# The second half of a two-layer vision tower: another layout of attention, work moved from VectorE to ScalarE, gelu over pairs of banks

## What is computed

```python
# layer 1, after the first layer's attention and mixture of experts
h = h + attn(layernorm(h))       # 16 heads of 16, causal, no softmax:
    att = where(causal, q @ k.T / sqrt(16), -inf)
    att = (where(att > 0, att**2 + 1, 0) + where(-100 <= att <= 0, 1 - att/100, 0)) / 1000
    y = (att @ v) @ W_proj
h = h + ffn(layernorm(h))        # ternary weights w_up (1024x256), w_down (256x1024)
    up = gelu(rms_norm(x) @ ternary(w_up).T)
    out = rms_norm(up) @ ternary(w_down).T
```

## Time and profile before

| | us |
|---|---|
| median of 3 runs | 829.77 (825.41 to 830.24) |
| the profiled execution | 828.23 |
| its span, first to last instruction | 826.2 |
| busy: TensorE | 713.3 (86%) |
| busy: VectorE | 645.6 (78%) |
| busy: ScalarE | 406.4 (49%) |
| busy: GpSimd | 86.4 (10%) |

### The profile page before, as it was taken

The page is one execution under the profiler, slowest core; times in us unless marked ns, Lnnn a source line. Parts: engine busy times, 40 slices in busy tenths (PEclk is TensorE's granted clock), DMA queues, the critical chain, the costliest instruction groups (busy, mean ns, idle before and its releaser), DMA issues.

```text
span 826.2 us, 25282 instructions
## 1 busy us (share of the span) xinstructions
PE 713.3 (86%) x10749; PEld 508.4 (62%) x10749; DVE 645.6 (78%) x1444; ACT 406.4 (49%) x609; POOL 86.4 (10%) x76
## 2 busy tenths in 40 slices
PE   4878999999999999858776889999999988988756
PEld 3565767666666767545574566666666756655634
DVE  6677979797978788786596589888888998686753
ACT  4536464545555554543213573828456481745413
POOL 1100212121212120100000000010101010010000
PEclk9889999999999999957855999999999999999969
DMA  8033202020202002000000000000000000000000
GB/s 306 35 138 118 77 0 76 0 76 0 76 0 76 0 0 103 3 1 1 2 0 2 2 2 27 2 28 2 25 0 0 25 2 26 2 28 2 28 0 27
DMA packets 7532, 27.24 MB, mean 33 GB/s; under 512 B 2480, under 2 KB 3376, under 8 KB 5936
## 3 DMA queue, kind: packets, MB, share of 16 engines
q1 hardware_dynamic: 7472, 26.35, 8.7%
HBM read 22.16 MB, written 4.19 MB: 32 GB/s over the span
## 4 chain that ended last, share of the span: by engine, by line
PE 51%; DVE 24%; issue 10%; ACT 9%; SPq 2%; DMA 2%; POOL 1%; DVEq 0%; POOLq 0%; ACTq 0%
PE PS L374 8%; PE PS L753 6%; PE PS L323 5%; PE PS L385 5%; PE PS L718 4%; PE PS L484 4%; PE PS L364 4%; PE PS L473 3%; DVE mx L1308 3%; DVE Pm L1314 3%; PE PS L428 2%; ACT w_s L1029 2%; PE PS L695 2%; PE PS L709 2%; DVE work L1700 2%
## 5 line engine op out<-in xcount | busy, mean ns | idle before, releaser
L904 ACT ACTIVATE PT<-PS 128x512 f32<-128x512 f32 x64 | 36.8, 596 | 71.5 <-PE PS L473 71.5
L364 PE MATMUL PS<-ident_s,xn 128*128 128x128 f32 x256 | 48.1, 305 | 25.9 <-DVE xn L1229 22.7
L731 PE MATMUL PS<-xT,wqkv_h 128*128 128x512 f16 x256 | 63.8, 394 | 6.0 <-ACT w_s L1029 4.5
L323 PE MATMUL PS<-tokW_h,w_s 128*128 128x256 f16 x504 | 58.5, 273 | 0.0
L897 ACT ACTIVATE Pm<-Pm 128x1024 f32<-128x1024 f32 x32 | 33.1, 1054 | 46.5 <-DVE Pm L1314 46.5
L364 PEld LDWEIGHTS PS<-ident_s,xn 128*128 128x128 f32 x256 | 31.1, 149 | 38.4 <-DVE xn L1229 20.7
L323 PEld LDWEIGHTS PS<-tokW_h,w_s 128*128 128x128 f16 x504 | 48.7, 98 | 5.8
L753 PE MATMUL PS<-tokW_h,work 128*128 128x256 f16 x448 | 51.4, 273 | 0.3 <-issue 0.3
L374 PE MATMUL PS<-xT,wat_h 128*128 128x512 f16 x192 | 46.2, 400 | 4.5 <-DVE xT L1618 4.5
L731 PEld LDWEIGHTS PS<-xT,wqkv_h 128*128 128x128 f16 x256 | 22.7, 100 | 44.1 <-ACT w_s L1029 18.0
L473 PE MATMUL PS<-ident_s,Pm 128*128 128x128 f32 x256 | 42.5, 305 | 6.7 <-DVE Pm L1314 6.4
(11 more groups left out here) (248 smaller groups left out, 1605.7 us busy)
## 6 DMA issues: line engine op xcount, KB each, us to landing
work<-in_x SPq DMA_DIRECT2D x7, 1536.0 KB, 6.5
out<-H SPq DMA_DIRECT2D x8, 512.0 KB, 2.6
w_s<-in_w SPq DMA_DIRECT2D x3, 1024.0 KB, 7.0
work<-in_x SPq DMA_DIRECT2D x3, 512.0 KB, 6.1
wup_s<-in_wup SPq DMA_DIRECT2D x1, 1024.0 KB, 5.8
wdn_s<-in_wdn SPq DMA_DIRECT2D x1, 1024.0 KB, 7.9
w_s<-in_tokW SPq DMA_DIRECT2D x3, 256.0 KB, 4.5
wup_s<-in_wqkv SPq DMA_DIRECT2D x1, 768.0 KB, 7.5
```

The source lines that it names most:

```text
L323: m = pe.matmul(dst, halves_[xi][:, k, rows], w[:, wi, k, cols], start=(n == 0), stop=(n == 3 * chunks - 1))
L364: m = pe.transpose(PS[:, bank, t * P:(t + 1) * P], xn[:, t, c * P:(c + 1) * P], ident_s[:, :])
L731: m = pe.matmul(PS[:, UP_BANKS[f % 3], :], wup_h[:, c, f * P:(f + 1) * P], part[:, c, :], start=(k == 0), stop=(k == 2 * C - 1))
```

## The change

- Attention: keys are stored once (kT), the queries twice with zeros (qM), in the buffers exchanged. Scores are 32 rows by 64 columns (image_scores, as in the first half), with 128 moving columns; partitions are (image of the tile, key). The mask is 16 small matmuls a tile with the same tiles (keyb, cmaskb). Value products have depth 64, 64 for each pair of tiles in place of 32, into banks 4 and 5 by image. The value projection is one product of 128x256 a tile and pass.
- VectorE pieces on ScalarE: norm3 for slots 1 to 7 becomes a_norm3 (Identity with bias -mean*rstd and scale rstd; VectorE makes the bias, minus_mean3), turned becomes a_turned, the keys of v_B1 go to a_B1_k. ScalarE has them behind lins(g, 3), and the second a_turned behind the queries.
- silus(g) moves to slot g+1, behind minus_mean3.
- TensorE's down products of tiles 0 and 1 run their high halves ahead of the grams, their low halves behind them, all four tile halves in bank 7 (down_part).
- Gelu, copy and low half go over two banks at a time (1024 elements) for blocks 0 to 5, and singly for 6 and 7; four up banks in place of three.
- Setup: cmask comes in eight small loads at the end of loads_B in place of one at its head; setup_B makes keyb by a memset and two reductions in place of one copy.

```diff
-        UP_BANKS = (4, 7, 5)
+        UP_BANKS = (6, 7, 4, 5)
...
-        loads_B = [(cmask_s, cmask), (eb_s, eb), (rev8_s, rev8), (ridx_s, ridx), (iota_s, iota64),
+        loads_B = [(eb_s, eb), (rev8_s, rev8), (ridx_s, ridx), (iota_s, iota64),
...
+        loads_B += [(cmask_s[32 * i:32 * i + 32, :, 0:L], cmask[32:64, :, :]) for i in range(4)]
+        loads_B += [(cmask_s[32 * i:32 * i + 32, :, L:96], cmask[0:32, :, 0:32]) for i in range(4)]
...
             def turn2(g, last):
                 if last:
-                    pe.wait_ge(Bq_out, 2)
+                    pe.wait_ge(Bq_out, 4)
...
             def B2_scores(g, t):
-                for i in range(4):
-                    pe.matmul(PS[:, i, hb:hb + 256], identb[:, :], cmaskb[:, :, :], start=True, stop=False,
-                              skip_group_check=True)
-                for b in range(2):
...
-                            m = pe.matmul(PS[:, i, hb + c * P + b * L:hb + c * P + (b + 1) * L],
-                                          kB[r, c, 2 * t + b, :, :], qT[r, c, at:at + L],
-                                          start=False, stop=True, tile_position=(32 * i, 0), skip_group_check=True)
-                m.then_inc(Bs_mm, 1)
+                for upper in (True, False):
+                    qs = slice(0, L) if upper else slice(0, 32)
+                    at = slice(0, L) if upper else slice(L, 96)
+                    for b in range(2):
+                        for i in range(4):
+                            r = slice(32 * i, 32 * i + 32)
+                            masked = PS[b * L:(b + 1) * L, i, hb:hb + 256].rearrange("p (h q) -> p h q", q=L)
+                            pe.matmul(masked[:, :, qs], keyb[r, int(upper), :], cmaskb[r, :, at], start=upper,
+                                      stop=False, tile_position=(32 * i, b * L), skip_group_check=True)
+                image_scores(t, kT, qM, hb).then_inc(Bs_mm, 1)
...
             def B2_values(g, pair):
+                    for c in range(C):
+                        for e in range(2):
+                            for b in range(2):
+                                for i in range(4):
...
+                                    m = pe.matmul(PS[32 * i:32 * i + 32, 4 + b, to:to + L],
+                                                  V2[rows, t, 4 * i + 2 * c + e, :], F[rows, t % 2, at:at + L],
+                                                  start=(e == 0), stop=(e == 1), tile_position=(b * L, 32 * i),
+                                                  skip_group_check=True)
...
             def B3_up(g, nxt):
-                    if f >= 3:
-                        pe.wait_ge(g_ok, NF * g + f - 2)
+                    if f == 4:
+                        pe.wait_ge(g_ok, 5 * g + 1)
+                    elif f == 6:
+                        pe.wait_ge(g_ok, 5 * g + 2)
...
             def slot_B(g, prev, nxt, routed=None):
                 if prev:
-                    pe.wait_ge(g_ok, NF * g)
+                    pe.wait_ge(g_ok, 5 * g)
+                    for t in (0, 1):
+                        down_part(g - 1, t, G_hi, True)
                     for f in range(NF):
                         gram(g - 1, f)
-                    B3_down(g - 1, (0, 1))
+                    for t in (0, 1):
+                        down_part(g - 1, t, G_lo, False)
...
+            def a_norm3(g):
+                act.wait_ge(nm3_ok, g)
+                for t in range(TILES):
+                    act.activation(xn1[:, t, :], H[:, TILES * g + t, :], ACT.Identity, bias=nm3[:, t:t + 1],
+                                   scale=rstd[:, t:t + 1]).then_inc(xn3_ok, 1)
+            def a_turned(g, pair):
+                act.wait_ge(Y_mm, TILES * g + 2 * pair + 2)
+                act.activation(yT[:, 2 * pair:2 * pair + 2, :, :].rearrange("p t c (b q) -> p b (t c) q", b=2),
+                               PS[:, 4:6, 0:E].rearrange("p b (n q) -> p b n q", q=L), ACT.Copy, scale=1e-3)\
+                   .then_inc(yT_out, 1)
...
             def a_B3(g, nxt):
                 if nxt:
                     relus(g + 1, 0)
+                for p in range(NF // 2):
+                    gelus(g, p)
+                    if p == 0 and nxt:
                         relus(g + 1, 1)
                         lins(g + 1, 0)
+                    if p > 0:
+                        g_high(g, p - 1)
+                g_high(g, NF // 2 - 1)
...
             def slot_B(g, prev, nxt, routed=None):
                 if nxt:
+                    a_norm3(g + 1)
+                a_turned(g, 0)
+                if nxt:
                     a_B1_x(g + 1)
...
                     a_B1_q(g + 1)
+                a_turned(g, 1)
...
-                turned(g, 0, 4)
-                if nxt:
-                    norm3(g + 1)
+                if nxt:
+                    minus_mean3(g + 1)
                 if routed in ("batch", "last"):
+                    silus(g - 1)
                     weighted_hots(g)
...
-                if nxt:
-                    v_B1(g + 1)
                 stats4(g, 0)
-                turned(g, 1, 4)
...
-                if routed in ("first", "batch"):
-                    silus(g)
                 if nxt:
                     v_quads(g + 1, 0)
                     v_quads(g + 1, 1)
                     v_lin(g + 1)
-                g_parts(g, 0, 4)
+                g_parts(g, (0, 1))
                 if nxt:
                     poly(g + 1, 0)
-                g_parts(g, 4, NF)
+                g_parts(g, (2, 3))
                 if nxt:
                     poly(g + 1, 1)
```

More of the change, by code:

```diff
@@ L745, in gram, with down_part @@
                     m.then_inc(ss_mm, 1)
+            def down_part(g, t, part, high):
+                for f in range(NF):
+                    if high and t == 0 and (f % 2 == 0 or f == NF - 1):
+                        pe.wait_ge(gh_out, 5 * g + (f // 2 + 1 if f < NF - 1 else 5))
+                    m = pe.matmul(PS[:, 7, t * E:(t + 1) * E], part[:, f, t * P:(t + 1) * P], wdn_h[:, f, :],
+                                  start=(high and f == 0 and t == 0), stop=(not high and f == NF - 1),
+                                  skip_group_check=True)
+                if not high:
+                    m.then_inc(dn_mm, 1)
             def B3_down(g, tiles):
@@ L981, in a_B1_k @@
             def a_B1_k(g):
[L982 to L985 removed]
+                for c in range(C):
+                    act.wait_ge(Bk_mm, 2 * g + c + 1)
+                    act.activation(kT[:, c, :], PS[:, 4 + c, :], ACT.Copy, scale=1 / WS).then_inc(Bk_out, 1)
             def a_B1_q(g):
@@ L1016, in quads, with g_two, gelus, g_high @@
                 act.activation(v, v, ACT.Square).then_inc(quad_ok, 1)
-            def g_high(g, f):
-                act.wait_ge(g_ok, NF * g + f + 1)
-                act.activation(G_hi[:, f, :], g32[f], ACT.Copy).then_inc(gh_out, 1)
+            def g_two(p):
+                return [(g32_two[p].rearrange("p (f n) -> p f n", f=2), G_hi[:, 2 * p:2 * p + 2, :])] if p < g_pairs\
+                    else [(g32[f], G_hi[:, f, :]) for f in (6, 7)]
+            def gelus(g, p):
+                act.wait_ge(up_mm, NF * g + 2 * p + 2)
+                if p == 0 and not first(g):
+                    act.wait_ge(gl_out, 5 * g)
+                if p < g_pairs:
+                    act.activation(g_two(p)[0][0], PS[:, 6 - 2 * (p % 2):8 - 2 * (p % 2), :], ACT.Gelu).then_inc(g_ok, 1)
+                else:
+                    for f in (6, 7):
+                        act.activation(g32[f], PS[:, f - 2, :], ACT.Gelu).then_inc(g_ok, 1)
+            def g_high(g, p):
+                for n, (part, high) in enumerate(g_two(p)):
+                    act.wait_ge(g_ok, 5 * g + p + n + 1)
+                    act.activation(high, part, ACT.Copy).then_inc(gh_out, 1)
             def a_B3(g, nxt):
```

142 lines of the change are left out of this document (62 added, 80 removed).

## The result

The changed kernel took 846.89 us (median of 4 runs, 845.61 to 850.44) beside 827.59 for the kernel before on the same chip: ratio 1.0225, 95% interval 1.0185 to 1.0264. The forecast was 837.0, its range 815 to 846. The profiled execution took 846.12, its span is 844.0.

The account below looks back on a forecast made before the run. TensorE looked like the bound, but a ring of waits through TensorE, VectorE and ScalarE was taken to set the slots. Terms of +2.1 on 828.23 gave 830.3, clock drops +6.5, so 837; range 815 to 846.

Parts of the forecast that it names:

- ring: Second half: cycle of waits through TensorE, ScalarE and VectorE from one slot's scores to the next; batch slots 48.2 us at full clock.
- Scores: First scores pair of a slot: 1.7 us instead of 3.18, so -1.5 a slot at seven boundaries.
- gelu by pairs: ScalarE's relu 1 waits behind a two-bank gelu, 2.95 instead of 1.60; second polynomial's end +1.6 us at seven boundaries.
- t0: End of a slot's first scores pair, the instant from which the prediction gives its times.
- F1: Instant when VectorE's second polynomial is out and the next statistics start; predicted at 17.1 us after t0, before 15.49.
- Norm, values, rest: Normalization on ScalarE: +0.35 us in six slots, about +0.4 in the last; value products and what follows: +0.2, seven times.
- The clock: TensorE's new 2.45 us gap behind the value products brings half clock: 1.3 us, five drops, +6.5, bounds 0 and 8.
- High-first: 0: High down halves ahead of the grams fill TensorE's wait for low halves; costed at 0, as value products wait anyway.
- the second pair ... saves nothing: A slot's second scores pair gets shorter too but ends in a wait for F1, so no saving was counted.
- Small tiles: Rival: small value matmuls run one behind the other, 2.1 us a pair instead of 1.2; 844 us, chance 0.12.
- The clock holds: Rival: no clock drop behind the new gap after the value products; 830 us, no change to be seen, chance 0.28.

Follow-up runs that it names:

- e3: Changed kernel with gelu, its copy and its low half for one bank at a time again; 833.1 us, ratio 1.0071.
- e2: Changed kernel with the low passes of the down products of tiles 0 and 1 behind the first value pair instead of ahead; 836.8 us, ratio 1.0102.
- e15: Kernel before with only the new attention layout, keys on ScalarE and setup, plus 8 useless 512-column products ahead of and between the grams; 827.2 us, ratio 0.9991.
- e1: Changed kernel with 20 useless products behind the first value pair of slots 1 to 6; 836.9 us, ratio 1.011.
- e10: Kernel before with only the new attention layout, keys on ScalarE and the setup; 837.2 us, ratio 1.0117.
- e8: Changed kernel with the down products of tiles 0 and 1 behind the grams again, high and low passes together; 835.5 us, ratio 1.0095.
- e18: The e16 kernel without its 8 useless products a slot; 824.4 us, ratio 0.996.
- e4: Changed kernel with the next slot's normalization on VectorE again; 830.1 us, ratio 1.0024.
- e16: Changed kernel with single gelu, down products behind the grams, early statistics and normalization for slots 2 to 7, and 8 wide useless products; 816.5 us, ratio 0.9875.
- e14: Changed kernel with single gelu, down products behind the grams, early statistics and normalization from slot 0 on, and 24 narrow useless products; 825.7 us, ratio 0.9971.

## Why the prediction was right in its ring and wrong in its sum

**Scores, gelu by pairs: right.** 1.70 for the pair, relu 1 at t0 + 2.94 (2.95), F1 at t0 + 16.99 (17.1); e3 gives the 1.54 back.

**Norm, values, rest: near, a little short.** e2's slot of 48.61 at full clock stands against 48.2 predicted. A norm took 0.49 (2.08 for four, pitched) where 0.45 stood, a value pair 1.54 to the next product where 1.2 stood, with a bound of 2.2. Some 0.4 a slot, 2.5 us in six (in e15, with the layout alone, 0.7 a slot). No key wait is left ahead of the second value pair. The cited rule of the Trainium skill ("TensorEngine Tiling (Array Packing)", "Instruction Overhead") would have these 128 records take 3.2 us by the prediction's estimate; they took 1.60, 12.5 ns each, so the measurement goes against the page here.

**The clock: the step that failed.** "I take 1.3 ... I count five drops: +6.5, bounds 0 and 8." The gap came as predicted (2.54 for 2.45) and the half clock behind it, but in all six slots, and in four of them for most of 8 us instead of one stretch of 4 at 0.65. Against e2 it cost slots 2 to 6 some 1.5, 2.2, 2.4, 4.2 and 3.4 us, and against e1 it cost slot 1, which has half clock in e2 too, 1.7: 15.4 in all, outside the bounds. With 15.4 for 6.5 and the 2.5 above, the forecast would have been 837.0 + 8.9 + 2.5 = 848.4, near the 846.9 measured. The bounds came from one row at one place, where other work followed. Here 0.53 of a batch slot's 2.2 us fell on the stretch up to the projection and 1.69 on the projection, all on the ring. Slots 5 and 6 paid for a second stretch, which the prediction did not have, behind waits of 2.15 and 2.42 us that the gap has no part in. In slot 5, TensorE's timeline, first of the changed kernel, then of e2:

```profile
714.36 5.31 PE L647 MATMUL PS<-w_s,gT 128*8 128x256 f32 x16 [2.15 <-DVE gT L1646]
```

```profile
707.01 3.62 PE L647 MATMUL PS<-w_s,gT 128*8 128x256 f32 x16 [2.15 <-DVE gT L1647]
```

Nor did allow a limit between 2.12 and 2.24 us to be read from them: in slot 0 of the kernel before a wait of 2.07 stands ahead of half clock (timeline and window):

```profile
450.52 7.03 PE L374 MATMUL PS<-xT,wat_h 128*128 128x512 f16 x24 [2.07 <-DVE xT L1618]
```

```profile
452.00:456.00 4.00, 4.00 (x14) 1.61 (x13) 3.97 (x5) 1.00 (x2) 0.00 (x0) 0.68 0.00 0
```

**"High-first: 0", and "the second pair ... saves nothing": the hidden half of the same error.** As terms of the ring both hold as far as the runs show. But both take work from where TensorE waits for VectorE or move it, and neither was priced in clock. The layout alone, worth -11.6 by the terms, cost 9.1 (e10), and 8 useless products undid the loss, but did not bring the -11.6 (e15). High passes first moved the idle stretch from ahead of the grams, where the half clock is mostly covered (e8), to behind the value products, where nothing covers it. So the prediction's account, in which the gap came from the pairs and the norm, was too narrow: in the kernel before the longer scores kept TensorE busy where e10 waits, and the edits that shorten or move TensorE's work opened a stretch somewhere, each in its own place (e10, e8, the changed kernel).

**The rivals.** "Small tiles" named 844 but for value pairs of 1.8 or more; they took 1.54, so its nearness is chance. "The clock holds" would have needed e1's or e2's order.

## What to carry to other kernels

Where TensorE is the busiest engine but the ring runs through others, work taken from TensorE can turn into idle time, and idle time into half clock on the products behind it: ask of every saving where the new wait stands and what runs after it. Before trusting such a saving, put a few useless wide products into the wait; if the time falls, the clock is the likely cost, and moving real work there a cure. Price a clock drop by all the work that follows on the path until the clock is back, in each pass of the loop, and read it slot by slot: the same kernel can have it in one slot and not in the next.

## What the runs showed of the hardware

- A wait need not be long: 1.38 us followed by thin grams was enough for 0.66 and 0.63 (e10, e18). Nor does its length decide. In slot 2 of e18 the same 1.38 us and the same grams have full clock behind them (32 down passes in 3.69), a wait of 2.05 had half clock behind it in some slots and not in others (e4), and slot 5's wait of 2.15 us for gT, the same in all 20 kernels here, has half clock behind it in 11 profiles and full clock in 9. What decides is left open. At 1.7 us for each such stretch (5.31 for 3.62, above), differences of 2 or 3 us between two of these kernels can be that alone.
- TensorE can stand at the return of its loop with no releaser in the trace. With 833 (changed kernel) and 841 (e16) matmul records in a slot of the loop there is no such stall; with 853 (e1) it is 2.39 and 1.85 us, with 857 (e14) 3.00 and 2.92. The number, the width and the place of the added products changed together; what lies behind it was not tried.
- Useless products of 128x512 cost TensorE 0.25 us each (five in 1.25, e15) and the kernel less than nothing: VectorE and ScalarE set the pace there.
